# Routed expert stages of two layers: chunks of 256 slots against chunks of 128 slots placed by a table

## What is computed

```python
def _L2_ffn_ref(x, gate_w, gate_b, w1, b1, w2, b2, ln_g, ln_b):   # E = 8, F = 512, TOP_K = 2
    logits = (x @ gate_w + gate_b) / TEMP
    keep = one_hot(top_k(logits, TOP_K)[1], E).any(-2)
    gate_probs = softmax(where(keep, logits, -inf))
    h = gelu(einsum('bsd,edf->bsef', x, w1) + b1)
    expert_out = einsum('bsef,efd->bsed', h, w2) + b2
    out = einsum('bse,bsed->bsd', gate_probs, expert_out)
    ...
def _L3_ffn_ref(x, Wr, W1, W3, W2):                               # E = 8, F = 512, cap = 1280
    top_v, top_i = top_k(clip(xf @ Wr, -CLAMP, CLAMP), 2)
    ...
    kept = pos < cap
    h = silu(einsum('ecd,edf->ecf', xe, W1)) * einsum('ecd,edf->ecf', xe, W3)
    ye = einsum('ecf,efd->ecd', h, W2)
    out = zeros((T, D)).at[tokens].add(wk[:, None] * yp)
```

## Time and profile before

| | |
|---|---|
| median of three runs | 1562.0 us (1555.54 to 1562.56) |
| the profiled execution | 1558.36 us, of it the span 1556.6 us |
| mean granted clock of TensorE | 0.895 |
| busy: PE, DVE, ACT, POOL | 77%, 60%, 47%, 55% |
| l2e on PE | 791.33 to 944.02 us |
| l3e on PE | 1288.19 to 1523.71 us |

### The profile page before, as it was taken

One profiled execution on the slowest core, in us unless ns is written; L12 is line 12 of the kernel. 1 busy time (PEld: TensorE's weight loads), 2 busy tenths in 40 slices (PEclk: granted clock), 3 DMA queues, 4 the chain that ended last, 5 costly groups with the idle time before them and its releaser, 6 DMA issues.

```text
span 1556.6 us, 36184 instructions
## 1 busy us (share of the span) xinstructions
PE 1195.8 (77%) x11766; PEld 971.0 (62%) x11766; DVE 937.5 (60%) x2743; ACT 735.8 (47%) x1807; POOL 854.4 (55%) x1119
## 2 busy tenths in 40 slices
PE   2888882954888779776269995898889839999991
PEld 1666661943667557565169994576667627888881
DVE  3788881227999867688612223788788733444444
ACT  2677660323888635465124445676555512222223
POOL 1366764434777423547744555678888862333334
PEclk9999995985999979887579997999999959999996
DMA  5222302643333192201358884000001012222216
GB/s 144 96 102 93 97 13 81 189 127 101 107 110 110 43 396 82 74 6 52 102 163 227 229 222 120 2 3 13 16 18 58 19 39 61 66 65 70 70 38 166
DMA packets 156862, 147.35 MB, mean 95 GB/s; under 512 B 21899, under 2 KB 129181, under 8 KB 156705
## 3 DMA queue, kind: packets, MB, share of 16 engines
q1 hardware_dynamic: 134560, 118.87, 26.0%
q0 software_dynamic: 11264, 21.07, 4.0%
q10 hardware_dynamic: 10880, 5.41, 1.4%
HBM read 89.77 MB, written 57.87 MB: 95 GB/s over the span
## 4 chain that ended last, share of the span: by engine, by line
PE 32%; DVE 7%; POOL 7%; issue 6%; ACT 4%; DMA 2%; SPq 0%; POOLq 0%; ACTq 0%; DVEq 0%
PE l2e_ps_y L1298 5%; PE l3e_ps_y L1298 5%; PE l2e_ps_h L1284 5%; PE l3e_ps_h L1288 4%; PE l3e_ps_h L1289 3%; POOL l_rows_in L1077 2%; PE l3a_ps_ym L2395 2%; PE l3a_ps_kv L2324 1%; PE l3a_ps_q L2308 1%; DVE l3e_hT L1342 1%; ACT l3e_sT L1318 1%; POOL l3a_cms L2217 1%; DVE x L684 1%; PE l3a_ps_t L2356 1%; PE l2e_ps_x L1274 1%
## 5 line engine op out<-in xcount | busy, mean ns | idle before, releaser
L1368 POOL DMA_INDIRECT l_rows_out<-l3e_y,l3e_target x80 | 77.7, 971 | 166.6 <-DVE l3e_y L1356 149.5
L1318 ACT ACTIVATE l3e_sT<-l3e_ps_h 128x256 f32<-128x256 f32 x160 | 61.3, 383 | 187.7 <-PE l3e_ps_h L1289 152.2
L1342 DVE TENSOR_TENSOR l3e_hT<-l3e_sT,l3e_ps_h 128x256 f32<-128x256 f32 x160 | 67.4, 421 | 99.1 <-ACT l3e_sT L1318 99.1
L1315 ACT ACTIVATE l2e_hT<-l2e_ps_h,l2e_b 128x256 f32<-128x256 f32 x160 | 69.9, 473 | 113.4 <-PE l2e_ps_h L1284 111.4
L1368 POOL DMA_INDIRECT l_rows_out<-l2e_y,l2e_target x80 | 77.7, 972 | 83.2 <-DVE l2e_y L1354 66.8
L1288 PE MATMUL l3e_ps_h<-l3e_xT,l3e_w 128*128 128x256 f32 x320 | 100.6, 396 | 5.2 <-DVE l3e_hT L1342 0.9
L1289 PE MATMUL l3e_ps_h<-l3e_xT,l3e_w 128*128 128x256 f32 x320 | 96.1, 382 | 0.0
L1077 POOL DMA_INDIRECT l_rows_in<-l2a_rt_rows,l2f_slot x64 | 66.0, 1031 | 40.6 <-ACT l2a_rt_rows L919 22.9
L1298 PE MATMUL l2e_ps_y<-l2e_w,l2e_hT 128*128 128x128 f32 x640 | 78.9, 277 | 0.1
L1284 PE MATMUL l2e_ps_h<-l2e_xT,l2e_w 128*128 128x256 f32 x320 | 77.6, 386 | 0.6 <-DVE l2e_xT L1333 0.6
L1298 PE MATMUL l3e_ps_y<-l3e_w,l3e_hT 128*128 128x128 f32 x640 | 78.0, 275 | 0.0
(11 more groups left out here) (525 smaller groups left out, 3701.8 us busy)
## 6 DMA issues: line engine op xcount, KB each, us to landing
l2e_w<-in_L_ffn_w SPq DMA_DIRECT2D x80, 256.0 KB
l_rows_in<-l1f_empty SPq DMA_DIRECT2D x34, 528.0 KB, 6.5
l1a_side<-in_fside_Bx16xSxS SPq DMA_DIRECT2D x32, 512.0 KB, 3.6
l0e_w<-in_L_ffn_w SPq DMA_DIRECT2D x32, 256.0 KB, 3.1
l_rows_in<-l0a_fill_rows SPq DMA_DIRECT2D x14, 528.0 KB, 2.8
l_rows_out<-l0a_fill_rows SPq DMA_DIRECT2D x12, 512.0 KB
l3e_w<-in_L_ffn_W SPq DMA_DIRECT2D x24, 256.0 KB
l2e_rows<-l_rows_in ACTq DMA_DIRECT2D x40, 132.0 KB
```

What stands on the lines that cost most here:

```text
L1315: nc.scalar.activation(hT[:, b, f, :], ps_h[f][:, 0:CHUNK], act_func, **bias).then_inc(sems["h_ready"], 1)
L1318: nc.scalar.activation(sT[:, f % 2, :], ps_h[f % 2][:, 0:CHUNK], act_func).then_inc(sems["s_ready"], 1)
L1342: nc.vector.tensor_tensor(hT[:, b, f, :], sT[:, f % 2, :], ps_h[2 + f % 2][:, 0:CHUNK], ALU.mult).then_inc(sems["h_ready"], 1)
L1368: pool.indirect_dma_start(out=r.rows_out, out_offset=bass.IndirectOffsetOnAxis(ap=target[:, c % 2, a:a + 1], axis=0), in_=y[:, c % 2, a, : ...
```

## The change

Both expert stages go to a new function, `slotted_programs`, with 71 chunks of 128 slots (`SLOTS`): the first 128 slots of each of the eight experts at fixed places (8 chunks, no table), and 63 more (`MORE_CHUNKS`), whose expert and base stand in the tables. Layer 3 therefore gets a table too: its `Router` now runs `totals` on PE and `allot` on DVE at the end of l3a. The arithmetic of `allot` now runs over 63 entries, and each expert's count is lowered by 128 first (and cut at the capacity in layer 3).

Every chunk loads all of its matrices, w1 (w3) and w2, in a ring of six (`ROWS`); there is no set that serves five chunks any more. w2 is laid out on the host so that a partition's part is one piece of 2 KB. The biases of layer 2 are loaded once for all experts (L2 only); ACT and DVE pick theirs by reading the expert from the table in each of the 63 chunks. SP issues all loads of the rows. The first six chunks' weights are issued before the rows are awaited, in layer 2 before the table is there. The twelve loads for l3a now come behind the whole of l2e in SP's order. All loops are written out. There is one more 528 KB part of the empty table to fill in l0a.

```diff
+SLOTS = P
+MORE_CHUNKS = 2 * T // SLOTS - 1
...
+        self._step(dve, V.tensor_scalar(self.counted[:, :], self.counted[:, :], float(-SLOTS), None, ALU.add))
...
+    def sync(sp, rows_ready, allotted):
+        def load_first(q):
+            e, k = expert_of(sp, q), q % ROWS
+            freed(sp, "h_ps", (q - ROWS + 1) * FC)
+            sp.dma_start(w1[:, k, :], w1_dram[e, :, :]).then_inc(sems[f"in{k}"], 16)
+            if w3 is not None:
+                sp.dma_start(w3[:, k, :], w3_dram[e, :, :]).then_inc(sems[f"in{k}"], 16)
+            freed(sp, "y_ps", q - ROWS + 1)
+            sp.dma_start(w2[:, k, :], w2_dram[e, :, :]).then_inc(sems[f"in{k}"], 16)
+
+        for q in range(ROWS):
+            load_first(q)
+        rows_ready(sp)
+        for q in range(N):
+            if q == E:
+                sp.wait_ge(allotted, 1)
+            if q >= ROWS:
+                load_first(q)
+            if q < E:
+                tile = r.rows_in[q * stride:q * stride + SLOTS, :]
+            else:
+                first = sp.value_load(r.chunk_base[0:1, q - E:q - E + 1], min_val=0, max_val=r.rows_in.shape[0] - SLOTS)
+                tile = r.rows_in[bass.ds(first, SLOTS), :]
+            freed(sp, "y_ready", 2 * (q - ROWS + 1))
+            sp.dma_start(rows[:, q % ROWS, :], tile).then_inc(sems[f"in{q % ROWS}"], 16)
...
+        def turn(q):
...
+            passed(pe, f"in{q % ROWS}", per_chunk * (q // ROWS + 1))
+            freed(pe, "xT_ready", q - 1)
+            nc.tensor.transpose(ps_x[q % 2][:, 0:SLOTS], rows[:, q % ROWS, 0:D], core.ident[:, :]).then_inc(sems["xT_ps"], 1)
...
+        turn(0)
+        for q in range(N + 1):
+            for f in range(FC):
+                hidden(q, f)
+                product(q - 1, f)
+                if f == 0:
+                    turn(q + 1)
...
+    def scalar(act, allotted):
...
+            if b1 is not None:
+                if q == E:
+                    act.wait_ge(allotted, 1)
+                e = expert_of(act, q)
...
+            passed(dve, "y_ps", q + 1)
+            if b2 is not None:
+                e = expert_of(dve, q)
+                nc.vector.tensor_tensor(y[:, q % RING, :], ps_y[q % 2][:, 0:D], b2[:, columns(e, D, 0, D)], ALU.add).then_inc(sems["y_ready"], 1)
...
@@ -2736,16 +2957,14 @@
-            sp.wait_ge(allotted, 1)
-
-            def load_weights(sp):
-                pairs_done(sp)
-                weights(sp)
-            expert.sync(sp, rows_ready=rows_in, behind_first=load_weights)
+            expert_weights(sp)
+            expert.sync(sp, rows_in, allotted)
+            pairs_done(sp)
+            weights(sp)
             all_stored(sp)
...
+    "L2_ffn_w2": lambda a: a.reshape(a.shape[0], -1, P, a.shape[2]).transpose(0, 2, 1, 3).reshape(a.shape[0], P, -1),
```

More of the change, by code:

```diff
@@ L51, in __init__ @@
         self.tables = {}
-        for layer, slots, top in (("l0", T, 1), ("l2", 8 * L2_STRIDE + CHUNK, 2), ("l3", MAX_SLOTS, 2)):
+        for layer, slots, top in (("l0", T, 1), ("l2", 8 * L2_STRIDE + CHUNK, 2), ("l3", MAX_SLOTS + FILL * P, 2)):
             self.tables[layer, "in"] = nc.dram_tensor(f"{layer}_rows_in", (slots, ROW), F32).ap()
@@ L763, in __init__ @@
         self.weigh = sb("weigh", [P, NT, E]) if top == 1 else None
-        if cap is None:
-            NC = MAX_SLOTS // CHUNK
+        self.allots = top > 1
+        if self.allots:
+            NC = MORE_CHUNKS
             self.starts_i, self.starts = sb("starts_i", [P, NC], I32), sb("starts", [P, NC])
@@ L801, in prepare @@
         pool.memset(self.running[:, 0, 0, :], 0.0).then_inc(s["consts"], 1)
-        if self.cap is None:
-            pool.iota(self.starts_i[:, :], [[CHUNK, MAX_SLOTS // CHUNK]], base=0, channel_multiplier=0).then_inc(s["filled"], 1)
+        if self.allots:
+            pool.iota(self.starts_i[:, :], [[SLOTS, MORE_CHUNKS]], base=0, channel_multiplier=0).then_inc(s["filled"], 1)
         pool.wait_ge(s["consts"], 6)
@@ L1120, in allot @@
         self._step(dve, V.tensor_tensor(self.line[:, :], self.line[:, :], self.starts[:, :], ALU.add))
[L1121 removed]
+        self._step(dve, V.tensor_scalar(self.line[:, :], self.line[:, :], float(SLOTS), float(E * self.stride), ALU.add, ALU.min))
         V.tensor_copy(r.chunk_base[:, :], self.line[0:1, :]).then_inc(s["allotted"], 1)
@@ L2701, in psum_free @@
         pe.wait_ge(router.s["pos_read"], NT // 4)
-    return Programs(None, tensor, scalar, vector, gpsimd), weights, prepare, psum_free, router.scattered
+        pe.wait_ge(router.s["allotted"], 1)
+    return Programs(None, tensor, scalar, vector, gpsimd), weights, prepare, psum_free, router.scattered, router.s["allotted"]
 def pairs_to_end(nc, core, a, r2, r3, out):
@@ L2721, in pairs_to_end @@
         combine.allocate_rows(arrivals)
+        cap = -(-T * 2 * 5 // (8 * 4))
         own = Part(phase, "l3a", "left")
-        attention, weights, prepare, attention_psum_free, rows_sent = linear_programs(
+        attention, weights, prepare, attention_psum_free, rows_sent, third_allotted = linear_programs(
             nc, core, own, combine, 3, a["L3_xattn_Wq"], a["L3_xattn_Wkv"], a["L3_xattn_null_kv"], a["L3_xattn_ln_q_g"],
             a["L3_xattn_ln_q_b"], a["L3_xattn_ln_out_g"], a["L3_xattn_ln_out_b"], a["L3_xattn_Wout"],
-            r3, a["L3_ffn_Wr"], -(-T * 2 * 5 // (8 * 4)), 7)
+            r3, a["L3_ffn_Wr"], cap, 7)
         own.release_psum()
         arrivals.release()
-        third, third_stored, _, _ = expert_programs(nc, core, Part(phase, "l3e", "right"), r3, 8, MAX_SLOTS // CHUNK // 8, a["L3_ffn_W1"], a["L3_ffn_W2"],
-                                                 ACT.Silu, w3_dram=a["L3_ffn_W3"], earlier=used)
+        third, third_weights, third_stored, _, _ = slotted_programs(
+            nc, core, Part(phase, "l3e", "right"), (None, None), r3, cap, a["L3_ffn_W1"], a["L3_ffn_W2"],
+            ACT.Silu, w3_dram=a["L3_ffn_W3"], earlier=used)
         own.release()
@@ L2747, in _ @@
             sp.wait_ge(combine.s["added"], combine.NQ)
-            third.sync(sp, rows_ready=rows_sent)
+            third.sync(sp, rows_sent, third_allotted)
             third_stored(sp)
@@ L2764, in _ @@
             pairs.scalar(act)
-            expert.scalar(act)
+            expert.scalar(act, allotted)
             attention.scalar(act)
-            third.scalar(act)
+            third.scalar(act, third_allotted)
             last.scalar(act)
@@ L2773, in _ @@
             combine.shift(dve)
-            expert.vector(dve)
+            expert.vector(dve, allotted)
             attention.vector(dve)
-            third.vector(dve)
+            third.vector(dve, third_allotted)
             last.vector(dve)
```

159 lines of the change are left out of this document (149 added, 10 removed).

## The result

The changed kernel takes 1586.2 us (median of four runs, 1582.87 to 1593.08) beside 1562.3 us for the kernel before (four runs, 1555.54 to 1562.57): a ratio of 1.0169, 95% interval 1.0125 to 1.0214. It is slower, by 1.3 to 2.1%. The forecast was 1584 us. In a second comparison, on one chip, the ratio was 1.0178 (1.0161 to 1.0196). The profiled execution after is 1587.64 us, its span 1585.9 us, at a mean granted clock of 0.891.

A forecast was written before the change was run, and what follows sets the result against it. SP's issues and table reads were taken to bound both expert stages. The profiled 1558.4 us + 34 (L2 stage) + 3 (l3a's moved loads) - 12 (L3 stage) = 1583; forecast 1584 us, range 1558 to 1622.

The forecast's parts named there:

- SP as the bound: In both expert stages SP's issues and table reads, not PE, set the pace of a chunk; 69%.
- The size of SP's chunk: SP's issues and two table reads per chunk take 2.81 us in l2e and 3.29 us in l3e.
- The read step: One table read on SP, from the end of one issue to the next, costs 0.83 us, mean of four samples.
- the stages cancel: Rival for both expert stages: a read step of 0.77 takes 15 us off, to 1569 us; chance 12%.
- my sum: Whole kernel: profiled 1558.4 us, +34 for L2, +3 for l3a's moved loads, -12 for L3, giving 1583.
- Transfers at zero: In the expert stages transfers add nothing; at 271 GB/s they would add 6 us in all, kept for the range.
- The L2 stage: Layer 2's expert stage, followed in order of time, gets 34 us longer, with PE idle for a third of l2e.
- The moved loads of l3a: Loads now behind the whole L2 stage on SP delay the wqT copy and the combine: +3 us.
- The rival of the falling clock: In the expert stages a lower granted clock makes PE slower than SP; 10% for more than 30 us.
- The L3 stage: Layer 3's expert stage, followed in order of time, ends at 1516.3 us instead of 1528.6: -12 us.
- The table's arithmetic: Layer 3's table work on VectorE is hidden ahead of the last scatter; up to 9 us if scatters were faster.
- The last step of the sum: From 1583 us to the forecast of 1584, with the median of the runs 3.6 us above the profiled execution.

The follow-up runs named there:

- the mix: L2 as in the kernel before, L3 in 71 chunks of 128 with rows by ACT: 0.9748 of the kernel before (1557.7 us), again 0.9778 (1524.6 us).

## Why the prediction was right, and where it was not

**SP as the bound** held in both stages, shown from three sides: a read less and the rows elsewhere speed it up, a read more slows it down, and half the bytes leave the pace as it was.

**The size of SP's chunk** came out right, 2.82 and 3.34 us against 2.81 and 3.29, but by luck and not by its own terms. The read step was 0.76 us, not 0.83: the mean of four samples had one of 0.96 in it, and the one of the running stage, 0.85, belonged to the loop of the kernel before. The load behind w1 costs 0.10 + 0.38 where I had 0.05 + 0.43, the same sum. The regular chunk is thus 2.67 and 3.15 us. What filled the place of my surplus of 0.14 is irregular: now and then an issue takes 0.6 to 2.1 us instead of 0.35, which is 0.10 us a chunk in l2e and 0.15 in l3e, and in l3e SP waits 4.7 us for y_ps over these chunks (3.0 us of the first wait come ahead of them). The rival "the stages cancel" had the condition right, a step of 0.76 or 0.77, and the time wrong, since neither it nor my sum had a term for long issues. By the regular chunk alone the sum gives 1566, 9 us less in each stage.

The Trainium skill (DMA: Bandwidth & Descriptors, section Latency and other measured facts) has a floor of some 600 ns for `tensor_load`. The 63 loads of L1450 on SP in l2e show otherwise (ns, min/median/max):

```profile
L1450 SPq TENSOR_LOAD <-l2f_chunk_expert x63: 264/270/487, 792.2 to 967.8; - x63
```

**Transfers at zero** held: 234 and 274 GB/s at shares of 0.77 and 0.86 are 304 and 319 GB/s at full share, where I kept 271 for the range.

**The L2 stage**: +34 forecast, +34.8 measured, and PE idle for between a fifth and a quarter of it behind the rows, not a third (36.4 of 160 us).

**The moved loads of l3a**: +3 forecast for the combine's start. The copy of wqT came 7.2 us behind the last scatter's issue instead of 5.4, +1.9:

```profile
975.64 4.49 DMA l3a_nv<-in_L_xattn_null_kv
...
986.62 0.59 ACT L2654 COPY l3a_wqT<-l3a_ps_t 128x512 f32<-128x512 f32 x1 [8.76 <-PE l3a_ps_t L2488]
```

The chain of waits runs through the landing of l3a_nv, as forecast. The attention lost 2.7 us more behind that, which I had not in the sum, and a lower granted clock goes with it. The stretch of 20 us that begins 33 us behind that scatter in either kernel, after and then before:

```profile
1013.00:1033.00 20.00, 16.81 (x193) 11.16 (x193) 13.09 (x37) 12.14 (x34) 14.03 (x16) 0.91 0.00 1
```

```profile
980.00:1000.00 20.00, 17.07 (x236) 11.71 (x235) 15.22 (x45) 13.43 (x37) 15.23 (x19) 1.00 0.01 2
```

Of fourteen profiles the seven with 0.90 to 0.93 in this stretch have 338.8 to 341.5 us between the stages; the seven with 0.97 or more have 335.4 to 339.5. That is a correlation, not a test: it explains a part, and no run took the clock alone. The rival of the falling clock did not come about in the expert stages (0.97 and 1.00).

**The L3 stage**: -12 forecast, -7.2 measured. From the first rows' issue (1321.69) to the last (1546.16) are 224.5 us, where my steps had 219.7 us (1284.6 to 1504.3): 3 us are the period's 0.05 x 63, the rest lies in the first chunks, where SP waits 3.0 us for y_ps once. The table's arithmetic was hidden as said, but barely: I had expected about 14 us to spare, as layer 2 has 17, and its last step on DVE stands only 2.3 us ahead of the last scatter's issue:

```profile
1317.10 0.18 DVE L1128 CAST l3f_chunk_base<-l3a_rt_line 1x63 int32<-1x63 f32 x1
```

So the mechanism was right, and that the total came within 2 us is in part luck: the L3 stage and the attention (5 and 2 us worse), the earlier start (2 better, cause open) and the medians (5 closer than the profiled runs) cancel nearly out. The last step of the sum was not clean either. 1583 stands for the profiled execution, which took 1588; with the 3.6 us between it and the median the forecast would have been 1587 and not 1584. Both are within 3 us of the 1586.2.

## What to carry to other kernels

Smaller chunks halve PE's work on padding (10240 slots worked on became 9088, for 8192 pairs) but double what the issuing engine does per slot. Before making a chunk smaller, add up the issues and table reads of one chunk on the engine that issues, at some 0.45 us a load and 0.76 us a lone read (0.54 more for a second one beside it), by these runs, and split them over two queues if the sum exceeds PE's chunk. The transfer share of 0.8 did not say who set the pace here: halving the bytes did. And look at the limit behind the first: with SP relieved, l2e in chunks of 128 came to transfers at a share of 0.94 and stayed 4.5 us longer than in chunks of 256 (169.5 against 165.0 us), while l3e gained over 35 us.

## What the runs showed that was not expected

**Long issues seem to come by count.** They often stand 19 to 21 loads apart. Of 18 such distances in the two stages of the changed kernel 8 are 19 to 21, 5 are 36 to 42, about twice that, and 5 are shorter. In its l3e they stand at 1408.03 and 1425.20 us, 20 issues later,

```profile
1408.03 1.55 SPq L1470 DMA_DIRECT2D l3e_w<-in_L_ffn_W  x1
...
1425.20 1.36 SPq L1470 DMA_DIRECT2D l3e_w<-in_L_ffn_W  x1
```

and in l2e with the added read 21 issues apart, though that is 24 us there:

```profile
958.20 1.47 SPq L1471 DMA_DIRECT2D l2e_w<-in_L_ffn_w  x1
...
982.15 1.40 SPq L1471 DMA_DIRECT2D l2e_w<-in_L_ffn_w  x1
...
1005.98 0.90 SPq L1471 DMA_DIRECT2D l2e_w<-in_L_ffn_w  x1
```

With half the bytes the distances are 19 to 21 again in 12 of 19 cases. With the rows by ACT they are fewer and less regular: in l3e 15 is the most frequent in SP's own issues, 20 with ACT's counted in. So the number of loads asked for fits better than time or bytes; that it is the cause was not shown, nor by what mechanism.

**PE's chunk in l3e** is 2.79 us when nothing stops it, where 2.9 was worked out from halves of the old one, and the DMA engines move 329 GB/s beside it at a share of 0.99.

**Chips differ by more than the change.** The kernel before took 1560 to 1565 us in three comparisons and 1594 to 1598 in two, and which of two versions is ahead went with it. In the mix 17 us of the difference lie ahead of the last scatter of layer 2's routing (798.2 against 781.5) and 16 in the old l2e's stage (180.6 against 165.0); the stretch between the stages and the L3 stage differ by 3 us together. No chip is known to stand in two of the comparisons, so it is not shown that the chip makes the difference.
